# A four-layer pre-norm decoder on one core: a bfloat16 key mask, VectorE's first blocks, a reordered depooling, a dense layer taken half by half, and the identity products placed anew

## The reference, cut to what matters

```python
x = x + L0_attn(ln(x))      # 16 heads of 8, rotary, causal
x = x + L0_xattn(ln(x))     # depooling: pooled context rows + ln(x) @ W_in
x = x + L0_ffn(ln(x))       # 8 experts, relu, top 2
x = x + L1_attn(ln(x))      # windowed attention, then a dense relu layer
x = x + L1_xattn(ctx, ln(x), mask)   # 8 heads of 16, 120 keys
x = x + L1_ffn(ln(x))       # 8 experts, gelu, top 2
x = x + L2_attn(ln(x))      # Mamba: convolution and scan
x = x + L2_xattn(ln(x), ctx)         # 16 heads of 64, a null key
x = x + L2_ffn(ln(x))       # weights rounded to three values, 1 shared + 8 experts
x = x + L3_attn(ln(x))      # 16 heads of 8, packed qkv
x = x + L3_xattn(ln(x))     # depooling again
x = x + L3_ffn(ln(x))       # 8 experts, relu, sigmoid gates
```

```python
logits = einsum('bhqd,bhkd->bhqk', Q, K) + b[0]
logits = logits + -1e30 * (1.0 - seq_mask[:, None, None, :])
weights = softmax(logits)
```

## Time and profile before

| | us |
|---|---|
| median of 3 runs | 1082.73 |
| lowest and highest | 1080.45, 1082.95 |
| profiled execution, its own time | 1083.21 |
| profiled execution, span from first to last instruction | 1081.2 |
| mean granted TensorE clock | 0.965 of full |

### The profile page before, as it was taken

The page is one execution under the profiler, slowest core; times in us unless marked ns, Lnnn a source line. Parts: engine busy times, 40 slices in busy tenths (PEclk is TensorE's granted clock), DMA queues, the critical chain, the costliest instruction groups (busy, mean ns, idle before and its releaser), DMA issues.

```text
span 1081.2 us, 17595 instructions
## 1 busy us (share of the span) xinstructions
PE 971.7 (90%) x6816; PEld 726.3 (67%) x6816; DVE 627.7 (58%) x1268; ACT 488.5 (45%) x1115; POOL 346.0 (32%) x443
## 2 busy tenths in 40 slices
PE   6899899999888999999588778899998998979998
PEld 4456789975566698994122224777777986659897
DVE  5576943267855762231699997555574558862322
ACT  1564344436523464344565462444434446715332
POOL 6850289534154300000066563321121006310000
PEclk9799899989989999999799899999999999999999
DMA  6700011000010001103000000100000000000111
GB/s 122 230 10 11 1 39 40 30 20 2 2 39 2 2 11 59 39 11 117 1 0 1 0 0 1 40 1 1 2 1 1 2 2 1 2 11 20 40 39 30
DMA packets 32268, 26.53 MB, mean 25 GB/s; under 512 B 3574, under 2 KB 28346, under 8 KB 31803
## 3 DMA queue, kind: packets, MB, share of 16 engines
q1 hardware_dynamic: 32187, 25.43, 8.1%
HBM read 24.89 MB, written 0.52 MB: 24 GB/s over the span
## 4 chain that ended last, share of the span: by engine, by line
PE 67%; DVE 23%; POOL 4%; issue 3%; ACT 2%; SPq 0%; DMA 0%; DVEq 0%; POOLq 0%; ACTq 0%
PE banks L856 19%; PE banks L836 14%; DVE work L1410 7%; PE banks L355 5%; PE banks L346 4%; DVE banks L1404 4%; PE banks L1577 3%; PE banks L1585 3%; PE banks L378 2%; DVE work L502 2%; PE banks L1636 1%; PE banks L1624 1%; PE banks L1599 1%; DVE keep L135 1%; PE banks L41 1%
## 5 line engine op out<-in xcount | busy, mean ns | idle before, releaser
L898 ACT ACTIVATE work<-banks,keep 128x512 f32<-128x512 f32 x236 | 157.0, 687 | 185.9 <-PE banks L836 185.7
L856 PEld LDWEIGHTS banks<-keep,work 128*128 128x128 f32 x1888 | 221.1, 192 | 5.4 <-DVE keep L972 0.5
L856 PE MATMUL banks<-keep,work 128*128 128x128 f32 x1888 | 221.9, 275 | 0.1
L972 DVE SCALAR_TENSOR_TENSOR keep<-banks,keep 128x128 f32<-128x128 f32 x256 | 72.1, 344 | 204.9 <-PE banks L856 204.6
L836 PE MATMUL banks<-rounded 128*128 128x512 f32 x672 | 174.6, 407 | 3.4 <-DVE rounded L947 2.7
L836 PEld LDWEIGHTS banks<-rounded 128*128 128x128 f32 x672 | 123.5, 192 | 30.7 <-DVE rounded L947 3.9
L670 ACT ACTIVATE work<-banks,work 128x128 f32<-128x128 f32 (+1 forms) x448 | 121.1, 388 | 42.8 <-DVE work L494 28.0
L149 POOL TENSOR_TENSOR keep<-keep 128x4 f32<-128x4 f32 x26 | 26.9, 1033 | 287.7 <-DVE keep L128 238.1
L1448 POOL TENSOR_TENSOR work<-work,keep 128x1024 f32<-128x1024 f32 x32 | 75.3, 2352 | 92.1 <-DVE work L1410 92.1
L494 DVE TENSOR_REDUCE work<-banks 128x8 f32<-128x1024 f32 (+1 forms) x64 | 69.1, 1080 | 51.2 <-PE banks L346 51.2
L1410 DVE TENSOR_TENSOR_SCAN work<-work,banks 128x1024 f32<-128x1024 f32 x32 | 73.2, 2286 | 1.1
(11 more groups left out here) (272 smaller groups left out, 1407.8 us busy)
## 6 DMA issues: line engine op xcount, KB each, us to landing
keep<-in_L_ffn_w_dram SPq DMA_DIRECT2D x32, 256.0 KB, 3.0
keep<-in_L_ffn_W_dram SPq DMA_DIRECT2D x16, 256.0 KB, 3.0
keep<-in_L_xattn_Wkv_dram SPq DMA_DIRECT2D x1, 2048.0 KB, 8.4
keep<-in_L_ffn_expert_w_dram SPq DMA_DIRECT2D x8, 128.0 KB, 2.6
keep<-in_L_ffn_expert_w_dram SPq DMA_DIRECT2D x1, 1024.0 KB, 7.2
keep<-in_halves_dram SPq DMA_DIRECT2D x1, 1024.0 KB, 9.2
keep<-in_L_attn_conv_w_dram SPq DMA_DIRECT2D x1, 1024.0 KB, 9.5
keep<-in_ctx_dram SPq DMA_DIRECT2D x1, 960.0 KB, 8.1
```

The costliest lines, as they stand in the source:

```text
L856: m = pe.matmul(k.ps[:, 4 + n % 2, j * P:(j + 1) * P], k.hT[n % 2][:, c, j * P:(j + 1) * P], w2[c], start=c == 0, stop=c == self.nf - 1)
L898: act.activation(k.hT[n % 2][:, c, :], k.ps[:, c, :], self.func, bias=bias, scale=scale)\
L972: ins = dve.scalar_tensor_tensor(acc[:, t, :], k.ps[:, 4 + n % 2, j * P:(j + 1) * P], k.w[:, 8 * t + e:8 * t + e + 1], acc[:, t, :], ALU.m ...
```

## The change

- The key mask becomes three bfloat16 parts in rows 0, 32 and 64 of `key16`, which add up to the float32 row; `three` has ones in these rows. The mask product is now one bfloat16 product of 96 rows. The mask is loaded three times (four more DMAs) and its parts are made on DVE beside items 6 and 8 of the relu experts, where before three instructions stood ahead of their first sum.
- In the first attention DVE takes over the boundary columns, the rotary sums of the first half and the blocks of sequence 0. The value products move behind the first scores (`project_v`), the transposed index behind the second projection, the context's statistics into steps 1, 3 and 5, and POOL's rotary sums of the second half behind the blocks of sequence 1.
- Depooling: the context's spreading is split in halves, with the transposes of the first norm half ahead of the picking columns; `n1.normal(1)` and `vector_scaled(0)` stand ahead of the first sum; the context's transposes go in halves into the places of identity products; the split of `L0_ffn`'s first weights moves one step later.
- POOL runs `bits.pool` ahead of `pool_pooled`, and waits for the dense layer's rounded input (`x_split`) before it prepares the sums' start.
- The dense layer's `layer2` of item 0 stands ahead of `layer1` of item 1; in `dense_sums` the next norm's first half stands ahead of `centre(1)`.
- The rounded experts' first sum stands ahead of routing, the exponentials behind the activation of item 3. The first blocks of the last attention stand ahead of the last statistics. In both projecting attentions the next norm's first half is one step later.
- Identity products: those of 16 and 12 in the first attention go; 3, then 2 ahead of each of four transposes, then 2, 3 or 5 stand in the other attentions' starts (1 to 5 before, or none); 3 in each of the last four steps of the last attention; 10, 12 and 10 ahead of the relu experts, the context attention and the gelu experts (7, 6 and 9 before); 11 in the dense layer go; 10 at item 3 in place of 18 at item 2 of the rounded experts.

```diff
@@ Turn
-    def tensor_half(self, pe, h):
+    def tensor_half(self, pe, h, bank=None, n=0):
         for b in range(4 * h, 4 * h + 4):
+            spin(k, pe, bank, n)
             pe.wait_ge(*self.norm.xn_ready.upto(b + 1))
@@ Attention.tensor
             self.project(pe)
-            spin(k, pe, 0, 16)
             k.arrived(pe, "masks")
...
         self.scores(pe, 0)
         if self.setup:
+            self.project_v(pe)
             pe.wait_ge(*self.turned_qk.upto(4))
...
-            if self.kind != "context":
-                spin(k, pe, 5 if self.proj else MB, 5)
-            self.turn.tensor_half(pe, 1)
+            spin(k, pe, PT0, 3)
+            self.turn.tensor_half(pe, 1, PT0, 2)
+            spin(k, pe, PT0, {"self": 2, "context": 3, "packed": 5}[self.kind])
...
-            if self.setup and s == self.STEPS:
-                spin(k, pe, 0, 12)
+            if self.kind == "packed" and s >= self.STEPS:
+                spin(k, pe, 2, 3)
@@ Attention.scores
-                pe.matmul(o, k.ones, bcast(k.key_row[:, b * M:(b + 1) * M], 1, self.per), start=True, stop=False)
+                pe.matmul(o, k.three, bcast(k.key16[:, b * M:(b + 1) * M], 1, self.per), start=True, stop=False)
@@ Attention.vector
         if self.kind == "rope":
-            self.keys(dve)
-            self.setup.vector_context(dve)
+            self.setup.vector_edges(dve)
+            self.keys(dve, 0)
+            self.rotated(dve, c, 0)
+            self.query_key_parts(dve, c, 0)
+            self.key_blocks(dve, 0)
+            self.keys(dve, 1)
...
+            if s in (1, 3, 5) and self.setup:
+                self.setup.vector_context(dve, s // 2)
...
-            if s == late + 9:
+            if s == late + (10 if self.proj else 9):
                 after.normal(dve, 0)
@@ Experts.tensor
-            if self.kind == "dense" and n == 0:
-                spin(k, pe, OB, 11)
+            if self.kind == "dense":
+                self.layer2(pe, n)
             if n + 1 < self.items:
                 self.layer1(pe, n + 1)
             elif tail is not None:
                 tail(pe)
-            self.layer2(pe, n)
+            if self.kind != "dense":
+                self.layer2(pe, n)
@@ Experts.layer2
-        if self.kind == "bit" and n == 2:
-            spin(k, pe, 7, 18)
+        if self.kind == "bit" and n == 3:
+            spin(k, pe, 7, 10)
@@ Experts.vector_start
         self.split_x(dve, 1)
+        if self.kind == "bit":
+            self.add(dve, 0, self.k.x)
         if self.routed:
             self.route(dve)
@@ the engines' blocks: TensorE, GpSimd
-            spin(k, pe, OB, 4)
+            setup.tensor_context(pe, 0)
             t1.tensor_half(pe, 1)
-            spin(k, pe, OB, 2)
             l0_cross.tensor_half(pe, 1)
-            setup.tensor_context(pe)
+            setup.tensor_context(pe, 1)
             t2.tensor_half(pe, 0)
             k.arrived(pe, "gates")
-            spin(k, pe, OB, 7)
+            spin(k, pe, OB, 10)
...
             n2.pool(pool)
+            bits.pool(pool)
             setup.pool_pooled(pool)
-            bits.pool(pool)
             n3.power(pool, 0)
             l1_attn.pool(pool, n4)
+            pool.wait_ge(*l1_dense.x_split.upto(2))
             for h in range(2):
                 l1_start.pool_half(pool, h)
@@ dense_sums; the depooling on VectorE
+                if h:
+                    n6.normal(dve, 0)
                 l1_after.centre(dve, h)
                 if h:
-                    n6.normal(dve, 0)
                     l1_cross.first_parts(dve)
...
-            l0_attn.vector(dve, n1, tail=lambda dve, j: l0_ffn.first_weights(dve) if j == 0 else None)
-            l0_cross.add(dve, 0)
+            l0_attn.vector(dve, n1, tail=lambda dve, j: l0_ffn.first_weights(dve) if j == 1 else None)
             n1.normal(dve, 1)
             setup.vector_scaled(dve, 0)
+            l0_cross.add(dve, 0)
```

More of the change, by code:

```diff
@@ L872, in scalar @@
             self.hidden(act, n)
+            if n == 3 and self.kind == "bit":
+                self.exponentials(act, 0, k.logit)
             if self.b2 and n == 3:
@@ L913, in split_x, with vector @@
         self.split(dve, self.k.xnT, self.x_high, self.x_low, h * HALF).then_inc(self.x_split.sem, 1)
-    def vector(self, dve, after=None, done=None):
+    def vector(self, dve, after=None, done=None, last=None):
         k, c = self.k, self.k.dchain
@@ L935, in vector @@
                 dve.wait_ge(*self.acc_done.upto(n + 1))
+                if h and last is not None:
+                    last(dve)
                 token_stats(k, dve, k.x, range(4 * h, 4 * h + 4))
@@ L2055, in vector_mask @@
         k.arrived(dve, "keys")
-        c.link(dve.tensor_copy(k.key_row[0:1, :], k.key_mask[:, :]))
-        c.link(dve.tensor_scalar(k.key_row[0:1, :], k.key_row[0:1, :], -1.0, -NEG, ALU.add, ALU.mult))
-        dve.tensor_scalar(k.key_row[0:1, :], k.key_row[0:1, :], k.key_b[0:1, 0:1], None, ALU.add)\
-            .then_inc(self.keyrow.sem, 1)
+        row = k.key_row[0:96, :]
+        c.link(dve.memset(k.three, 0.0))
+        for j in range(3):
+            c.step(dve.memset(k.three[32 * j:32 * j + 1, :], 1.0))
+        c.link(dve.tensor_copy(row, k.key_mask))
+        c.link(dve.tensor_scalar(row, row, -1.0, -NEG, ALU.add, ALU.mult))
+        c.link(dve.tensor_scalar(row, row, k.key_b[0:96, 0:1], None, ALU.add))
+    def vector_mask_parts(self, dve):
+        k, c = self.k, self.k.dchain
+        row = k.key_row[0:96, :]
+        c.link(dve.tensor_copy(k.key16, row))
[4 more added lines that the diff above has]
+        dve.tensor_copy(k.key16[64:96, :], row[64:96, :]).then_inc(self.keyrow.sem, 1)
 class BitWeights:
```

164 lines of the change are left out of this document (90 added, 74 removed).

## The result

The changed kernel takes 1050.71 us in the median of 4 runs (1049.33 to 1053.14), the kernel before 1082.84 in the median of 4: a ratio of 0.9705, 95% interval 0.9675 to 0.9734. The profiled execution took 1050.60 us, with a span of 1048.8 and a mean granted clock of 0.982 in place of 0.965.

What follows compares the result with a forecast made beforehand. TensorE's work, waits and clock were taken to bound the kernel (busy 90% of the span). Terms -8.9 -6.0 -2.5 -4.0 -2.0 -4.6 -1.8 +0.6 sum to -29.2, from 1083.2 to 1054.0 us; range 1042 to 1070.

Steps and rivals of the forecast that it cites:

- The mask: Context attention: bfloat16 mask products cut TensorE's work, steps fall from 2.54 to 2.00 us; -8.9 us, bounds -4 to -12.
- The first attention's start: VectorE takes over GpSimd's early work, first scores come at 23.3, 2.1 us of half clock regained; -6.0 us, -2 to -8.
- Depooling: End of first attention: output transpose waits less for VectorE, relu experts' layer 1 starts earlier; -2.5 us, 0 to -4.
- Relu experts: Normalisations no longer collide with GpSimd's `pool_pooled`; 2.0 us of waiting and three quarters of 2.7 go; -4.0 us, -2 to -4.7.
- Self attention's start: Eight added products in TensorE's waits recover 2.0 of 3.5 us lost to half clock; -2.0 us, 0 to -3.5.
- Dense layer: Faster normalisations, layer 2 of item 0 ahead, identity products gone, GpSimd's sums late next; -4.6 us, -2 to -6.5.
- Rounded experts: First sum ahead of routing lets TensorE start item 3's layer 2 at 844.9 instead of 846.70; -1.8 us, 0 to -2.5.
- last attention: Later GpSimd power at its start, partly offset by an earlier last output product at its end; together +0.6 us.
- the late power: Last attention's start: GpSimd's power and the blocks behind it come 1.5 us later, counted as +1.3 us, 0 to 1.6.
- the clock on the slow side: Rival: TensorE's clock falls in new gaps and stays, over context attention and 60 us of first, about 1100 us; chance 0.04.

Runs made afterwards that it cites:

- the copy first: Changed kernel with VectorE's copy of the turned weights ahead of output normalisation and residual, in the context attention alone: 1044.97 us in one run.
- the kernel with both collisions: Changed kernel with `pool_pooled` ahead of the rounding of weights again and without GpSimd's wait for the dense layer's rounded input: 1060.71 us, ratio 0.9770.
- the products alone: Kernel before with only the new identity products in later attention starts, the last attention's end and ahead of three stages: 1080.68 us, ratio 0.9950.
- the kernel with the early bias: Changed kernel with GpSimd's bias of the dense layer's sums between the self attention's two last powers: 1051.80 us in one run.
- the last kernel: Changed kernel with the context attention's copy first, last attention's first blocks behind the statistics, ten identity products in the first attention's start: 1042.71 us, ratio 0.9614.

## Why the prediction was right

The forecast named eight terms, and their sum, 29.2, is within 3.2 us of the 32.4 that the span gained. Part of that is luck: two terms were too large by 2.5 us together, and four too small by 5.6, of which 2.4 came for a reason that was not the forecast's.

- *The mask, 8.9, came as 7.3* (6.6 from the first scores). The mechanism is as put: TensorE set the step, VectorE does now. The product of 240 columns goes with its columns (0.21 to 0.31 for two, 0.25 taken). From the third scores to the last it is 26.1 us where it was 33.4, 7.3 of the 8.9 counted there. The end gives 1.5 back, 8.01 us behind the last scores where it was 6.50: 0.9 is the half clock from 343.72 on, since without it, as in the kernel with the dense layer's old order, the end takes 7.10. What bounds a step was mis-sized, as the order in VectorE's queue was not read: with the copy first the same work takes 1.92 a step. Undone, the mask gives back 5.4 in its stage.
- *The first attention's start, 6.0, came as 5.1.* The first scores, forecast at 23.3 and found at 23.35, and the third mask, at 29.9 and 29.37, are right. The clock gave back less: 10.24 us of half clock stayed of 13.65, where 2.1 of its 3 us had been counted as regained. In the kernels that kept the full clock the attention ended at 84.78 to 85.05, almost 9 us sooner than before, so this term depends on the clock more than its range of 2 to 8 says. With GpSimd's work undone it ends 5.4 later, the clock's part included.
- *Depooling, 2.5, came as 3.1*. It has no kernel of its own, so its cause is argued and not shown.
- *Relu experts, 4.0, came as 5.4.* The 2.0 us of waiting and the whole half-clock stretch went together; three quarters of 2.7 was the part mis-sized. The kernel with both collisions showed that the half-clock stretch returns with the collision.
- *Self attention's start, 2.0, came as 4.4*, and for another reason than put. The step that fails is that the eight added products keep the clock up: without them the stretch was gone too. With the products alone it was gone as well. What the two kernels share against the one before, other than where in time the stage lies, was not found. Each was profiled once, and the half clock in the first attention came and went with the code unchanged, so chance is not excluded: this cause stays open.
- *Dense layer, 4.6, came as 5.8.* By the undone kernels the products gained 1.4 from the order, 3.2 from the collision's waits and 2.4 from the clock, 7.1 in all. Behind them, from the last product to the first context maxima, 1.3 were lost: it is 14.1 us where it was 12.8, and 13.9 with the old identity products. The prediction's places had 6.4 and 1.8 for these two. The Trainium skill, "SBUF — State Buffer", section "Who interferes with whom", has a VectorE instruction with two SBUF inputs contend with GpSimd's reads; the centres, 1.13 us before and 4.24 now, agree. The prediction gave 1 us to this rule. The centres themselves grew by 3.1, but in the kernel with the early bias they were 2.1 shorter and the context attention's first scores came no sooner behind the last product.
- *Rounded experts 1.8 (1.9) and last attention +0.6 (+0.5)* are right. The kernel before had 3.4 us of half clock among the rounded experts and the changed one none, but that is not where the 1.9 come from: the last kernel has the same stretch there again and takes 59.19. Of the last attention +1.3 was put on the late power; undone it is 0.9.

Of the rivals, the clock on the slow side was given 0.04 and a price by the whole context attention. It is real: with the old products the changed kernel does exactly this in the context attention, and 14.9 of the 20 us that it gives back are there. So the forecast's weakest step was to cost the added products there at 1.3 us. They carry more than the mask does, and the mask without them is a loss in its own stage (55.84 us against 47.45). The prediction weighed this rival by the packed attention's steady steps; the clock fell in a wait in the stage's start, and did not rise in the steady steps behind it.

## What to carry to other kernels

Where work is taken from a busy TensorE, ask what its clock does in the new waits: a faster product and the identity products that fill the new waits are one change, and each measured alone can look like nothing or like a loss. When a second engine becomes the bound, read the order in its queue before its busy share; moving one copy ahead of work that nobody waits for gave 3.0 us here, and the same move cost 10 us, with the half clock that came along, where a transpose waited for what was moved back. Read stages, not only totals: the first attention ended anywhere from 85.00 to 89.69 us in kernels whose code there was the same.

## What the runs showed of the hardware

- TensorE stayed at 1.2 GHz for 51.2 us of the context attention, busy by the profile for 30.00 of 30.00 us in a window within; the clock rose at 362.07, 2.3 us before the attention's last output. The Trainium skill, "TensorE: Matmul & The Clock Gate", section "What's actually happening", has activity lift the slow clock; this stretch does not agree, and the measurement decides. Why it stayed was not tried.
- The first attention's start, the same code in nine kernels, ran with 0 to 13.7 us of half clock in the first 45 us, the first of it beginning anywhere from 23.41 to 29.69. The Trainium skill, "TensorE: Matmul & The Clock Gate", section "What's actually happening", calls the slow matmuls at a kernel's start variable from run to run for the same kernel; these profiles, of one run each, show such a variation at a later place.
- Four VectorE normalisations took 1.1 us alone and 4.2 to 5.4 beside GpSimd's tensor operations, in all four places shown here.
